# Far degree factors of every third chunk fetched from a table in HBM by GpSimd, in two of three sum stages of a graph kernel

## The chip, the cores and the metric

The program runs on one core of a Trainium2 chip. The metric is the device time of one execution in microseconds (us). The core has five engines with in-order instruction streams: TensorE (PE), VectorE (DVE), ScalarE (ACT), GpSimd (POOL) and SyncE (SP). SP issues plain DMAs; POOL issues the indirect ones (gathers and scatters by a list of row numbers). Engines wait for each other on semaphores.

## The reference

Two graph layers over 100000 nodes of 64 features and 25000 edges, sorted by destination. The part around the change is the second one, `_L1_gnn_ref`, called with `row = src`, `col = dst`:

```
for l in range(3):
    f1 = relu(x[row] @ nb_W[l] + nb_b[l]);  f2 = relu(x[col] @ self_W[l] + self_b[l])
    h = relu(concat([f1, f2]) @ att1_W[l] + att1_b[l])
    mask = clip(sigmoid(h @ att2_W[l] + att2_b[l]) * (ZETA - GAMMA) + GAMMA, 0, 1)
    rowsum = segment_sum(mask, row) + 1e-6
    d_inv_sqrt = clip(rowsum ** -0.5, 0, 10)
    vals = mask * d_inv_sqrt[row] * d_inv_sqrt[col]
    x = segment_sum(vals[:, None] * x[col], row)
    out = out + x
```

The factor `d_inv_sqrt[row]` is local to an edge once the edges stand in the order of `row`. `d_inv_sqrt[col]`, the far degree factor, stands at another place of the list and has to be looked up for each edge; where `col` has no edge of its own the factor is 10.

## The kernel before

The 25000 edges, padded to 25088, stand in 196 tiles of 128 edges, and four tiles make a chunk, so that there are 49 chunks (`NC1 = 49`, `C = 4`). For each of the three layers l = 0, 1, 2 there are three stages in a row:

- a dense stage (the matmuls of f1, f2 and h). For l = 1 and 2, POOL first gathers the rows of the last layer's `x`, 196 indirect DMAs at L1003, behind the semaphore `table`; the copy of the 100000 nodes to the output is done beside it in steps (`RUN_B`, `RUN_C`);
- a short chain for `rowsum` and its root, on 98 partitions by 256 places (`rowsum_dve`, L1206 to L1262). `DEGR` holds the 25088 degree factors by place. It is split at L1251 to L1259 into three bf16 parts, `TAB`, whose sum is the float;
- the sum stage (`aggregate_dve`), over the 49 chunks. The change lies here, for l = 0 and 1.

The sum stage looks the far factors up with TensorE. For each chunk c these steps follow one another:

- spread (SP, L1058): a DMA broadcasts the table row numbers of the chunk's 512 edges to all partitions, into one of two buffers `RB`;
- hot (ACT, L1355 and L1357): two activations turn them into a one-hot matrix `OH`, one of two buffers;
- bring (PE, L1451): 12 matmuls, four tiles by three parts, bring each edge's table row of 256 factors into PSUM;
- select (DVE, L1271): four instructions, one per tile, pick the column and leave the factor in `DCc`; the product with the near part is at L1274 (`VAL1`), and L1278 multiplies the chunk's feature rows by it (`Z`);
- turn_z (PE, L1461), scan (DVE, L1285, a running sum by segment), turn_back (PE, L1476), rows (ACT, L1348, a copy to SBUF) and store (SP, L1062, to HBM).

Each engine goes through its own list in order, with lags written out by `staged`: in step i, PE does bring(i), turn_z(i-2), turn_back(i-3); DVE does select(i), scan(i-2); ACT does hot(i), rows(i-4); SP does spread(i), store(i-5). So a spread stands behind a store on SP, and that store waits for rows, which stands behind a hot on ACT. In the first sum stage POOL does only one thing: it zeroes the chunk's part of `far` when the chunk is done (L999, 49 times); in the second and third sum stage before the change it has nothing there until the output scatters of the third (L1010). Below, T stands for the start of a chunk's select on DVE.

Of the kernel before, what the change touches and what calls it, by code (L numbers as in the profile page):

```python
# [9 lines left out]
ALU = mybir.AluOpType  # L10
# [17 lines left out]
C = 4  # L28
NCH = T // C
# [27 lines left out]
USE_DST = 0  # L57
NOROW = SL1 + 256
# [25 lines left out]
def build(nc, a, out):  # L84
    ctx = ExitStack()
    with ctx:
# [24 lines left out]
        row_d = dram("row_of_far_degree", (1, SL1), BF16)  # L111
        same_d = dram("same_as_before", (1, SL1), BF16)
# [863 lines left out]

        FORWARD, REVERSED = list(range(NC1)), list(range(NC1))[::-1]
# [7 lines left out]
        def L1_pool(g, top):  # L985
# [35 lines left out]
        def L1_sp(sp):  # L1021
# [31 lines left out]
            for l in range(LAYERS):  # L1053
                def spread(c, l=l):
                    b = c % 2
                    if l or c >= 2:
                        sp.wait_ge(signal("o_hot"), l * NC1 + c - 1)
# [13 lines left out]
                if l < 2:  # L1071
                    staged(NC1, [(0, spread), (5, store)])
# [133 lines left out]
        def rowsum_dve(v, l):  # L1206
# [42 lines left out]
            if l:  # L1249
                v.wait_ge(signal("o_mm"), NC1 * l)  # L1250
# [13 lines left out]
        def aggregate_dve(v, l):  # L1264

            def select(c):
                b = c % 2
                v.wait_ge(signal("o_mm"), l * NC1 + c + 1)
                for k in range(C):
                    u = C * c + k  # L1270
                    v.scalar_tensor_tensor(PICK[k], steps[:, :], far_c[:, u:u + 1], bank[2 + 2 * b + k // 2][:, (k % 2) * 256:(k % 2) * 256 + 256],  # L1271
                                           ALU.is_equal, ALU.mult, accum_out=DCc[:, u:u + 1])
                v.drain()  # L1273
# [34 lines left out]
        def L1_act(s_):  # L1308

            for l in range(LAYERS):  # L1310
# [39 lines left out]
                def hot(c, l=l):  # L1350
                    b = c % 2
                    s_.wait_ge(signal(f"o_ids{b}"), half_need(b, l, c))
                    if c >= 2:
                        s_.wait_ge(signal("o_mm"), l * NC1 + c - 1)
# [5 lines left out]
        def L1_pe(pe):  # L1360
# [27 lines left out]
            for l in range(LAYERS):  # L1388
# [53 lines left out]
                def bring(c, l=l):  # L1442
                    b = c % 2
# [3 lines left out]
                    if c >= 2:  # L1447
                        pe.wait_ge(signal("o_val"), l * NC1 + c - 1)
# [455 lines left out]
```

## Time and profile before

| | |
|---|---|
| median of 3 runs | 3198.88 us (3198.11 to 3206.03) |
| the profiled execution | 3199.13 us, span 3197.3 us |
| busy share of the span | DVE 69%, POOL 60%, PE 56%, PE weight load 45%, ACT 33% |
| chain that ended last | POOL 48%, issue 18%, DVE 13%, PE 12% |
| first sum stage | from about 2011 to about 2158 us |
| second sum stage | from about 2464 to about 2611 us |

The span is a sequence of stages with different limits, so these shares are an average. The chain of waits says which engine ended each stretch: POOL's indirect DMAs through the dense stages and the last sum stage, DVE through the first two sum stages, where its pieces return every 3 us. A row of a timeline gives start, duration, engine, line, operation, what it writes and reads, and in brackets how long its engine was idle before it and for whom.

### The profile page before, as it was taken

How to read it: one execution, taken by the hardware profiler on the slowest of the kernel's cores; microseconds unless marked ns; L12 is line 12 of the kernel's file. 1: busy time of each engine (PE TensorE's matmuls, PEld its weight loads, DVE VectorE, ACT ScalarE, POOL GpSimd, SP SyncE). 2: the span in 40 equal slices, each digit the busy share in tenths (PEclk: the TensorE clock that was granted, in tenths of full speed). 3: DMA queues.
4: the chain of work that ended last, by engine and by line, in shares of the span. 5: the costliest groups of instructions: out<-in, count | busy, mean ns of one | idle time of the engine just before them, and what ended most of it. 6: DMA issues, size and time to landing. Idle time of an engine off the chain costs nothing.

```text
span 3197.3 us, 34323 instructions
## 1 busy us (share of the span) xinstructions
PE 1780.0 (56%) x8972; PEld 1443.3 (45%) x8972; DVE 2195.2 (69%) x5951; ACT 1068.3 (33%) x2292; POOL 1913.7 (60%) x1844
## 2 busy tenths in 40 slices
PE   1124444441399986653665654665665656655663
PEld 0023333331299975542454433453444544544442
DVE  6748888887877744434555553897866988766775
ACT  0024444442144420001333323553444644443221
POOL 0057777777888017776777775017773017773776
PEclk9975555565555555556777776897888987787555
DMA  0023332231122212214222211233332333333543
GB/s 7 3 54 82 84 88 82 83 86 41 41 86 86 83 60 69 71 50 96 62 63 61 64 40 34 70 85 96 98 104 64 88 88 94 102 98 84 126 119 85
DMA packets 283933, 238.03 MB, mean 74 GB/s; under 512 B 161125, under 2 KB 207611, under 8 KB 283637
## 3 DMA queue, kind: packets, MB, share of 16 engines
q1 hardware_dynamic: 226933, 196.13, 21.4%
q0 software_dynamic: 56832, 40.05, 5.5%
q8 instruction: 58, 0.95, 0.1%
q14 instruction: 110, 0.90, 0.1%
HBM read 163.62 MB, written 84.20 MB: 78 GB/s over the span
## 4 chain that ended last, share of the span: by engine, by line
POOL 48%; issue 18%; DVE 13%; PE 12%; DVEq 4%; DMA 2%; SPq 1%; ACT 1%; POOLq 0%; ACTq 0%
POOL big L1003 13%; POOL G L994 12%; POOL regs L1845 7%; POOL out L1010 6%; POOL regs L1854 5%; PE bank L923 5%; POOL x_after_layer L647 5%; DVE den L1271 3%; PE bank L916 3%; DVE big L1285 2%; DVE big L1591 2%; PE bank L872 1%; DVEq L1590 1%; PE bank L1451 1%; DVEq L1273 1%
## 5 line engine op out<-in xcount | busy, mean ns | idle before, releaser
L1003 POOL DMA_INDIRECT big<-layer_rows,late x392 | 425.9, 1087 | 305.8 <-SPq L1075 186.9
L1845 POOL DMA_INDIRECT regs<-in_x,G x200 | 213.8, 1069 | 234.8 <-DVEq L1711 174.1
L1451 PE MATMUL bank<-regs,SQ 99*128 99x256 bf16 x1764 | 274.8, 319 | 84.2 <-ACT SQ L1357 77.7
L647 POOL DMA_INDIRECT x_after_layer<-G,idx_s x200 | 197.0, 985 | 198.0 <-DVEq L808 135.9
L1870 POOL DMA_INDIRECT farf<-dst_float,VAL x196 | 252.8, 1290 | 59.7 <-issue 59.7
L1451 PEld LDWEIGHTS bank<-regs,SQ 99*128 99x128 bf16 x1764 | 189.3, 112 | 152.8 <-ACT SQ L1357 102.7
L1010 POOL DMA_INDIRECT out<-G,scat_i x196 | 194.7, 993 | 104.4 <-issue 61.4
L1854 POOL DMA_INDIRECT regs<-in_x,G x200 | 211.2, 1056 | 70.2 <-issue 59.7
L1271 DVE SCALAR_TENSOR_TENSOR den<-steps,late,bank 128x256 f32<-128x256 f32 x588 | 245.2, 472 | 9.6 <-PE bank L1451 9.3
L994 POOL DMA_INDIRECT G<-x_after_layer,own_i x196 | 200.6, 1023 | 69.2 <-issue 61.0
L994 POOL DMA_INDIRECT G<-x_after_layer,far_i x196 | 198.5, 1013 | 66.5 <-issue 66.5
L505 PE MATMUL bank<-regs 128*128 128x196 bf16 x800 | 161.2, 356 | 90.8 <-ACT regs L492 90.8
L1355 ACT ACTIVATE SQ<-XC,row_of 128x512 bf16<-128x512 bf16 x147 | 105.9, 721 | 259.4 <-DMA XC<-row_of_far_degree 235.6
L1402 PE MATMUL bank<-ident,big 128*128 128x128 f32 x196 | 50.3, 347 | 226.8 <-DMA big<-layer_rows,late 226.8
L1398 PE MATMUL bank<-ident,XC 128*128 128x128 f32 x196 | 50.3, 408 | 215.2 <-DVEq L1114 215.2
L564 ACT ACTIVATE SQ<-XC 128x512 f32<-128x512 f32 x99 | 62.3, 629 | 284.8 <-DVE XC L547 284.7
L395 DVE RECIPROCAL dstat<-dstat 128x8 f32<-128x8 f32 (+1 forms) x196 | 38.9, 198 | 169.8 <-ACT dstat L408 169.8
L885 PE MATMUL bank<-ident,VS 128*128 128x128 f32 x100 | 32.6, 426 | 212.5 <-DVE VS L717 212.5
L933 PE MATMUL bank<-big,den 128*128 (+1 forms) x400 | 95.8, 420 | 93.4 <-DVE den L587 86.5
L1402 PEld LDWEIGHTS bank<-ident,big 128*128 128x128 f32 x196 | 23.2, 166 | 271.1 <-issue 270.9
L933 PEld LDWEIGHTS bank<-big,den 128*128 128x128 f32 x400 | 87.3, 322 | 106.7 <-issue 99.4
L1398 PEld LDWEIGHTS bank<-ident,XC 128*128 128x128 f32 x196 | 33.0, 206 | 226.0 <-issue 226.0
(416 smaller groups left out, 5745.7 us busy)
## 6 DMA issues: line engine op xcount, KB each, us to landing
regs<-x_after_layer SPq DMA_DIRECT2D x96, 256.0 KB, 3.2
out<-regs SPq DMA_DIRECT2D x96, 256.0 KB, 2.1
XC<-row_of_far_degree SPq DMA_DIRECT2D x147, 128.0 KB, 3.4
den<-in_x SPq DMA_DIRECT2D x50, 256.0 KB, 2.7
x_after_layer<-den SPq DMA_DIRECT2D x50, 256.0 KB, 2.0
regs<-tile_nodes SPq DMA_DIRECT2D x50, 256.0 KB, 3.2
layer_rows<-TS SPq DMA_DIRECT2D x98, 128.0 KB, 2.0
regs<-in_x SPq DMA_DIRECT2D x46, 256.0 KB, 2.8
```

The lines of the kernel that those rows point to most:

```text
L505: pe.matmul(o_, GE[b][h][:, k * P:(k + 1) * P], LT[:, h, part, :], start=(h + part == 0), stop=False)
L647: g.indirect_dma_start(x1_d, bass.IndirectOffsetOnAxis(ap=idx_s[:, b, k:k + 1], axis=0), G[:, b, k, 0, :], None, bounds_check=top, oob_is_ ...
L923: ins = pe.matmul(bank[4 + b][:, k * F:(k + 1) * F], ZTs[b][:, q * 512 + k * P:q * 512 + (k + 1) * P], wm[:, q, :], start=(q == 0), stop=( ...
L933: ins = pe.matmul(bank[b][:, k * F:(k + 1) * F], STg[b][:, k, :], big1[:, one(c, k), :].rearrange("p o f -> p (o f)"), start=True, stop=True)
L994: g.indirect_dma_start(G[:, b, grp // 2, grp % 2, :], None, x1_d, bass.IndirectOffsetOnAxis(ap=ix[:, u:u + 1], axis=0), bounds_check=top, ...
L1003: ahead(g, l, REVERSED, lambda u, l=l: g.indirect_dma_start(far[:, tile_of(u // C, u % C), :], None, xt_d[l - 1], bass.IndirectOffsetOnAxi ...
L1010: g.indirect_dma_start(out, bass.IndirectOffsetOnAxis(ap=scat_i[1][:, u:u + 1], axis=0), SUM[b][:, k, :], None, bounds_check=top, oob_is_e ...
L1271: v.scalar_tensor_tensor(PICK[k], steps[:, :], far_c[:, u:u + 1], bank[2 + 2 * b + k // 2][:, (k % 2) * 256:(k % 2) * 256 + 256], ALU.is_e ...
L1451: ins = pe.matmul(bank[2 + 2 * b + k // 2][:, (k % 2) * 256:(k % 2) * 256 + 256], OH[b][0:RB1 + 1, k * P:(k + 1) * P], TAB[0:RB1 + 1, part ...
L1845: g.indirect_dma_start(GR[:, c % DEEP, k, 0, :], None, a["x"], bass.IndirectOffsetOnAxis(ap=own0[:, c * C + k:c * C + k + 1], axis=0), bou ...
L1854: g.indirect_dma_start(GR[:, c % DEEP, k, 1, :], None, a["x"], bass.IndirectOffsetOnAxis(ap=far0[:, c * C + k:c * C + k + 1], axis=0), bou ...
L1870: g.indirect_dma_start(farf[:, u:u + 1], None, dstf_d, bass.IndirectOffsetOnAxis(ap=perm1[:, u:u + 1], axis=0), bounds_check=top, oob_is_e ...
```

## The change

For l = 0 and 1, chunks 5, 8, 11, ..., 47 (15 of the 49, `FETCHED`) are no longer looked up with TensorE. SP writes `DEGR` to a table in HBM once per layer (`table_out`, two DMAs behind `r_val`); POOL fetches from it by edge, with one indirect DMA of 128 single floats per tile (`fetch_degrees`, 60 per stage), at most three chunks in flight, and writes them into `DCc`. Places that have no factor keep the 10 that POOL writes there before. For a fetched chunk SP leaves out the spread, ACT the hot, PE the bring and DVE the four instructions of the select; the product at L1274 waits for the fetch (`pair0` to `pair2`) in place of the matmuls. The remaining 34 looked-up chunks alternate between the two buffers by a count of their own, `g`.

```
+FETCHED = [[c for c in range(NC1) if l < 2 and c >= 5 and c % 3 == 2] for l in range(3)]
+LOOKED = [[c for c in range(NC1) if c not in FETCHED[l]] for l in range(3)]
+LOOKED_BEFORE = [sum(len(LOOKED[k]) for k in range(l)) for l in range(4)]
...
+            def fetch_degrees(l):
+                g.wait_ge(signal("tables_out"), 16 + 32 * (l + 1))
+                for c in FETCHED[l]:
+                    i = fetch_index(l, c)
+                    landed = signal(f"pair{i % FARS}")
+                    if i >= FARS:
+                        g.wait_ge(landed, fetch_need(i - FARS))
+                    for u in range(C * c, C * c + C):
+                        g.indirect_dma_start(DCc[:, u:u + 1], None, deg_d, bass.IndirectOffsetOnAxis(ap=pos_i[:, u:u + 1], axis=0),
+                                             bounds_check=places, oob_is_err=False).then_inc(landed, 16)
...
+            for c in FETCHED[0]:
+                g.memset(DCc[:, C * c:C * c + C], 10.0)
+            g.drain()
+            fetch_degrees(0)
             for c in range(NC1):
                 g.wait_ge(signal("z_done"), c + 1)
                 g.memset(far[:, C * c:C * c + C, :], 0.0)
...
+                if l < 2:
+                    fetch_degrees(l)
...
+                def table_out(l=l):
+                    sp.wait_ge(signal("r_val"), l + 1)
+                    for h in range(2):
+                        sp.dma_start(at(deg_d, 256 * h, [[512, 49], [1, 256]]), DEGR[49 * h:49 * h + 49, :]).then_inc(signal("tables_out"), 16)
                 def spread(c, l=l):
-                    b = c % 2
-                    if l or c >= 2:
-                        sp.wait_ge(signal("o_hot"), l * NC1 + c - 1)
+                    if c not in LOOKED[l]:
+                        return
+                    g = LOOKED_BEFORE[l] + LOOKED[l].index(c)
+                    b = g % 2
+                    if g >= 2:
+                        sp.wait_ge(signal("o_hot"), g - 1)
...
-                    staged(NC1, [(0, spread), (5, store)])
+                    staged(NC1, [(0, spread), (1, lambda c: table_out() if c == 0 else None), (5, store)])
...
             def select(c):
                 b = c % 2
-                v.wait_ge(signal("o_mm"), l * NC1 + c + 1)
...
+                if c in FETCHED[l]:
+                    i = fetch_index(l, c)
+                    v.wait_ge(signal(f"pair{i % FARS}"), fetch_need(i))
+                else:
+                    g = LOOKED_BEFORE[l] + LOOKED[l].index(c)
+                    v.wait_ge(signal("o_mm"), g + 1)
...
                 def bring(c, l=l):
-                    b = c % 2
+                    if c not in LOOKED[l]:
+                        return
...
-                    pe.wait_ge(signal("o_hot"), l * NC1 + c + 1)
-                    if c >= 2:
-                        pe.wait_ge(signal("o_val"), l * NC1 + c - 1)
+                    pe.wait_ge(signal("o_hot"), g + 1)
+                    if i >= 2:
+                        pe.wait_ge(signal("o_val"), l * NC1 + LOOKED[l][i - 2] + 1)
```

The instruction streams show it on three engines. On VectorE, in the first sum stage (`den`, `late` and `VAL` are the buffers of the select and its product, `big<-big` or `big<-regs` the scan), from the select of chunk 4 on, before:

```order
L1271 SCALAR_TENSOR_TENSOR den,late<-steps,late,bank 128x256 [waits o_mm]
L1271 SCALAR_TENSOR_TENSOR den,late<-steps,late,bank 128x256 x3
L1274 TENSOR_TENSOR VAL<-late,VAL 128x4
L1278 TENSOR_TENSOR den<-big,VAL 128x256 [waits z_t]
L1285 SCALAR_TENSOR_TENSOR big<-regs,big,bank 128x256 [waits z_t,s_scan]
L1271 SCALAR_TENSOR_TENSOR den,late<-steps,late,bank 128x256 [waits o_mm]
L1271 SCALAR_TENSOR_TENSOR den,late<-steps,late,bank 128x256 x3
L1274 TENSOR_TENSOR VAL<-late,VAL 128x4
L1278 TENSOR_TENSOR den<-big,VAL 128x256 [waits z_t]
L1285 SCALAR_TENSOR_TENSOR big<-regs,big,bank 128x256 [waits z_t,s_scan]
```

and now, with chunk 5 in second place (the same instructions have the lines L1311, L1314, L1318 and L1325):

```order
L1311 SCALAR_TENSOR_TENSOR den,late<-steps,late,bank 128x256 [waits o_mm]
L1311 SCALAR_TENSOR_TENSOR den,late<-steps,late,bank 128x256 x3
L1314 TENSOR_TENSOR VAL<-late,VAL 128x4
L1318 TENSOR_TENSOR den<-big,VAL 128x256 [waits z_t]
L1325 SCALAR_TENSOR_TENSOR big<-regs,big,bank 128x256 [waits z_t,s_scan]
L1314 TENSOR_TENSOR VAL<-late,VAL 128x4 [waits pair0]
L1318 TENSOR_TENSOR den<-big,VAL 128x256 [waits z_t]
L1325 SCALAR_TENSOR_TENSOR big<-regs,big,bank 128x256 [waits z_t,s_scan]
```

The four selects of a fetched chunk are gone, and its product waits for `pair0`.

On SP, once the stage is full, a spread (the DMA into `XC`) and a store (the DMA to `layer_rows`) took turns before:

```order
L1062 DMA layer_rows<-TS 128x4x64 [waits q_out]
L1058 DMA XC<-row_of_far_degree 128x512 [waits o_hot]
L1062 DMA layer_rows<-TS 128x4x64 [waits q_out]
L1058 DMA XC<-row_of_far_degree 128x512 [waits o_hot]
L1062 DMA layer_rows<-TS 128x4x64 [waits q_out]
L1058 DMA XC<-row_of_far_degree 128x512 [waits o_hot]
```

and now:

```order
L1093 DMA XC<-row_of_far_degree 128x512 [waits o_hot]
L1097 DMA layer_rows<-TS 128x4x64 [waits q_out]
L1093 DMA XC<-row_of_far_degree 128x512 [waits o_hot]
L1097 DMA layer_rows<-TS 128x4x64 [waits q_out] x2
L1093 DMA XC<-row_of_far_degree 128x512 [waits o_hot]
L1097 DMA layer_rows<-TS 128x4x64 [waits q_out]
```

Two spreads in three steps remain, and the first of each pair stands behind two stores in place of one.

On ACT, a hot (two rows into `SQ`) and a rows (into `TS`) took turns. Now, from the hot of chunk 6 on, where a fetched chunk leaves two rows side by side:

```order
L1398 ACTIVATE SQ<-XC,row_of 128x512 [waits o_mm,o_ids0]
L1400 ACTIVATE SQ<-SQ,one_c 128x512
L1388 ACTIVATE TS<-bank 128x2x2x64 [waits q_stored1,s_bt]
L1388 ACTIVATE TS<-bank 128x2x2x64 [waits q_stored0,s_bt]
L1398 ACTIVATE SQ<-XC,row_of 128x512 [waits o_mm,o_ids1]
L1400 ACTIVATE SQ<-SQ,one_c 128x512
L1388 ACTIVATE TS<-bank 128x2x2x64 [waits q_stored1,s_bt]
```

The rows of every chunk keep their place behind a hot, while a third of the hots are gone.

## Rows read from the trace of the kernel before

**Rows 1.** Busy us (xcount) by stretch: PE, PEld, DVE, ACT, POOL; PEclk; DMA share; GB/s
```profile
2030.00:2140.00 110.00, 74.46 (x587) 57.01 (x584) 103.78 (x403) 66.08 (x110) 11.52 (x37) 1.00 0.39 89
2185.00:2425.00 240.00, 144.73 (x514) 106.71 (x513) 180.94 (x302) 103.65 (x257) 187.75 (x172) 0.84 0.33 100
2500.00:2600.00 100.00, 67.70 (x527) 52.30 (x525) 93.66 (x364) 59.84 (x99) 0.00 (x0) 0.98 0.38 88
2960.00:3160.00 200.00, 131.75 (x618) 91.76 (x616) 152.23 (x533) 54.84 (x76) 151.67 (x153) 0.56 0.49 123
```

**Rows 2.** Timeline of DVE, one chunk of the first sum stage
```profile
2071.06 0.45 DVE L1271 SCALAR_TENSOR_TENSOR den<-steps,late,bank 128x256 f32<-128x256 f32 x1
...
2072.80 0.16 DVE L1274 TENSOR_TENSOR VAL<-late,VAL 128x4 f32<-128x4 f32 x1
...
2074.06 0.45 DVE L1271 SCALAR_TENSOR_TENSOR den<-steps,late,bank 128x256 f32<-128x256 f32 x1
```

**Rows 3.** Timelines of PE, ACT and SP from the same point on
```profile
2071.19 0.44 PE L1476 MATMUL bank<-ident,big 128*128 128x128 f32 x2 [1.03 <-DVE big L1285]
2071.54 1.49 PE L1451 MATMUL bank<-regs,SQ 99*128 99x256 bf16 x12
...
2071.67 0.39 ACT L1348 ACTIVATE TS<-bank 128x256 f32<-128x256 f32 x1 [0.19 <-PE bank L1476]
...
2072.50 0.51 SPq L1058 DMA_DIRECT2D XC<-row_of_far_degree  x1
...
2075.93 0.72 ACT L1355 ACTIVATE SQ<-XC,row_of 128x512 bf16<-128x512 bf16 x1 [0.71 <-DMA XC<-row_of_far_degree]
```

**Rows 4.** Waits of ACT, 2010 to 2160 us: total, times, longest
```profile
ACT SQ L1355 <- DMA XC<-row_of_far_degree: 37.9, 41, 1.6
```

**Rows 5.** Timelines of ACT, PE and SP around a late spread
```profile
2142.54 0.72 ACT L1355 ACTIVATE SQ<-XC,row_of 128x512 bf16<-128x512 bf16 x1 [1.54 <-DMA XC<-row_of_far_degree]
...
2144.11 1.62 PE L1451 MATMUL bank<-regs,SQ 99*128 99x256 bf16 x12 [0.53 <-ACT SQ L1357]
...
2144.77 0.51 SPq L1058 DMA_DIRECT2D XC<-row_of_far_degree  x1
...
2148.25 0.72 ACT L1355 ACTIVATE SQ<-XC,row_of 128x512 bf16<-128x512 bf16 x1 [1.00 <-DMA XC<-row_of_far_degree]
```

**Rows 6.** Timelines of DVE and PE near the stage's start
```profile
2022.53 0.48 DVE L1271 SCALAR_TENSOR_TENSOR den<-steps,late,bank 128x256 f32<-128x256 f32 x1 [0.35 <-PE bank L1451]
...
2023.13 2.77 PE L1451 MATMUL bank<-regs,SQ 99*128 99x256 bf16 x12
...
2025.94 0.48 DVE L1271 SCALAR_TENSOR_TENSOR den<-steps,late,bank 128x256 f32<-128x256 f32 x1 [0.31 <-PE bank L1451]
...
2026.21 1.48 PE L1451 MATMUL bank<-regs,SQ 99*128 99x256 bf16 x12
```

**Rows 7.** POOL by line: busy us, mean ns, idle before
```profile
L1870 POOL DMA_INDIRECT farf<-dst_float,VAL x196 | 252.8, 1290 | 59.7 <-issue 59.7
L1003 POOL DMA_INDIRECT big<-layer_rows,late x187 | 204.0, 1091 | 57.0 <-issue 57.0
L999 POOL MEMSET big<- 128x256 f32 x49 | 15.3, 311 | 164.1 <-DVE den L1278 164.1
```

**Rows 8.** DVE by line and shape: first sum stage, then third
```profile
L1278 DVE TENSOR_TENSOR den<-big,VAL 128x256 f32<-128x256 f32 x30 | 12.7, 424 | 2.8
...
L1278 DVE TENSOR_TENSOR den<-big,VAL 128x256 f32<-128x256 f32 x40 | 17.2, 431 | 4.0 <-issue 0.4
```

**Rows 9.** DMA issues: KB each, median us to landing; first, then third stage
```profile
XC<-row_of_far_degree SPq DMA_DIRECT2D x31, 128.0 KB, 3.3
...
XC<-row_of_far_degree SPq DMA_DIRECT2D x40, 128.0 KB, 3.4
```

**Rows 10.** Timeline of DVE, end of the rowsum chain and first select
```profile
2006.21 0.42 DVE L1248 TENSOR_TENSOR den<-den 98x256 f32<-98x256 f32 x1
...
2011.41 0.48 DVE L1271 SCALAR_TENSOR_TENSOR den<-steps,late,bank 128x256 f32<-128x256 f32 x1 [2.42 <-PE bank L1451]
```

More of the change, by code:

```diff
@@ L111, in build @@
         row_d = dram("row_of_far_degree", (1, SL1), BF16)
+        deg_d = dram("degree_of_place", (SL1, 1))
         same_d = dram("same_as_before", (1, SL1), BF16)
@@ L975, in ahead_done, with fetch_index, fetch_need @@
                 eng.wait_ge(signal(f"ring{k}"), ROWS_IN + (16 * C) * ((use + 1) * len(range(k, NC1, RING))))
+        def fetch_index(l, c):
+            return l * len(FETCHED[0]) + FETCHED[l].index(c)
+        def fetch_need(i):
+            return 16 * C * (len(range(i % FARS, NCH, FARS)) + i // FARS + 1)
         FORWARD, REVERSED = list(range(NC1)), list(range(NC1))[::-1]
@@ L1249, in rowsum_dve @@
             if l:
-                v.wait_ge(signal("o_mm"), NC1 * l)
+                v.wait_ge(signal("o_mm"), LOOKED_BEFORE[l])
             v.tensor_copy(TAB[0:RB1, 0, :], DEGR)
@@ L1267, in select @@
                 b = c % 2
-                v.wait_ge(signal("o_mm"), l * NC1 + c + 1)
[L1269 to L1273, printed above, removed]
+                if c in FETCHED[l]:
[4 more added lines that the diff above has]
+                    v.wait_ge(signal("o_mm"), g + 1)
+                    for k in range(C):
+                        u = C * c + k
+                        v.scalar_tensor_tensor(PICK[k], steps[:, :], far_c[:, u:u + 1], bank[2 + 2 * (g % 2) + k // 2][:, (k % 2) * 256:(k % 2) * 256 + 256],
+                                               ALU.is_equal, ALU.mult, accum_out=DCc[:, u:u + 1])
+                    v.drain()
                 v.tensor_tensor(VAL1[:, C * c:C * c + C], DCc[:, C * c:C * c + C], VAL0[:, C * c:C * c + C], ALU.mult).then_inc(signal("o_val"), 1)
@@ L1350, in hot @@
                 def hot(c, l=l):
-                    b = c % 2
-                    s_.wait_ge(signal(f"o_ids{b}"), half_need(b, l, c))
-                    if c >= 2:
-                        s_.wait_ge(signal("o_mm"), l * NC1 + c - 1)
+                    if c not in LOOKED[l]:
+                        return
+                    g = LOOKED_BEFORE[l] + LOOKED[l].index(c)
+                    b = g % 2
+                    s_.wait_ge(signal(f"o_ids{b}"), 16 * (g // 2 + 1))
+                    if g >= 2:
+                        s_.wait_ge(signal("o_mm"), g - 1)
                     s_.activation(OFF[b], RB[b], ACT.Square, bias=row_of[:, 0:1])
@@ L1442, in bring @@
                 def bring(c, l=l):
-                    b = c % 2
+                    if c not in LOOKED[l]:
+                        return
+                    i = LOOKED[l].index(c)
+                    g = LOOKED_BEFORE[l] + i
+                    b = g % 2
                     if c == 0:
                         pe.wait_ge(signal("r_carry"), 2 * l + 2)
-                    pe.wait_ge(signal("o_hot"), l * NC1 + c + 1)
-                    if c >= 2:
-                        pe.wait_ge(signal("o_val"), l * NC1 + c - 1)
+                    pe.wait_ge(signal("o_hot"), g + 1)
+                    if i >= 2:
+                        pe.wait_ge(signal("o_val"), l * NC1 + LOOKED[l][i - 2] + 1)
                     for k in range(C):
@@ L1819, in _ @@
             top = g.to_reg(N - 1)
+            places = g.to_reg(SL1 - 1)
             for o in range(2):
@@ L1876, in _ @@
             L0_pool(g, top)
-            L1_pool(g, top)
+            L1_pool(g, top, places)
 mid_side, end_side = [], []
```

2 lines of the change are left out of this document (1 added, 1 removed).

## The prediction

> **What bounds the kernel now.** I read the busy time by stretch first, then the timelines of the five engines over two or three chunks, then the waits. In the first and second sum stage DVE is busy 94% of the time (103.78 of 110 us, 93.66 of 100) and TensorE's granted clock is 1.00 and 0.98, that is, 2.4 GHz nearly throughout [rows 1] (the stretches there are the first sum, a dense, the second sum and the third sum stage). One chunk takes DVE from 2071.06 to 2074.06, 3.00 us: 1.74 us for the select, up to the start of the product at 2072.80, and 1.26 us for the product, Z and the scan [rows 2]. The reader is to see in these rows that DVE has no gap to speak of, so that whatever leaves it counts at once. But ACT waits for the spread's DMA 41 times, 37.9 us in all [rows 4]: the next limit is near. The stages are passed in series (the dense stage starts on `table`, once the last store of the sum stage has landed), so a gain in a sum stage goes through to the end in full.
>
> **What the change removes.** For each fetched chunk DVE loses the 1.74 us of the select. Three chunks would then take 9.00 - 1.74 = 7.26 us. 15 fetched chunks in two stages make 30 x 1.74 = 52 us if DVE stayed the limit. That is the upper bound of the gain.
>
> **What is late next.** I follow the other engines' lists. Three loops matter, all prices at 2.4 GHz.
>
> Loop one, over three chunks. The spread of chunk c goes out on SP behind the store of c-6, and its rows waits for the scan that ends as the select of c-3 starts. From T at 2071.06, turn_back starts at 2071.19, rows at 2071.67, the spread goes out at 2072.50 (1.44 us after T), and its hot starts at 2075.93, 3.43 us later [rows 3]. From the start of a hot to that of its bring are 1.57 us (2142.54 to 2144.11) [rows 5], the bring takes 1.49 us [rows 3], and the select starts 0.04 us behind it (2023.13 + 2.77 = 2025.90 against 2025.94) [rows 6]. Sum: 1.44 + 3.43 + 1.57 + 1.49 + 0.04 = 7.97 us for three chunks. It is hidden today under 9.00, with 1.03 us to spare. Under 7.26 it isn't: the change leaves this loop as it is, since each looked-up chunk still stands behind the store of six chunks before.
>
> Loop two, over the hots. That same rows stands behind a hot on ACT, whose spread may be late. For the looked-up chunk that follows a fetched one, c-6's rows stands behind the hot of c-2. From that hot to this one it is 5.71 us where nothing else holds (2142.54 to 2148.25, through the rows, the store and the spread at 2144.77) [rows 5]. With the sequence looked A, looked B, fetched: B's hot starts at the earliest 1.44 + 3.43 = 4.87 us after the T of the B before; the next A's hot 5.71 us after it; that A's select 1.57 + 1.49 + 0.04 = 3.10 us later; the B behind it 3.00 us later. That is twice the period: 4.87 + 5.71 + 3.10 + 3.00 = 16.68 us, so 8.34 us for three chunks. The late spreads (5.71 already has one of 3.48) make me take 8.4.
>
> Loop three, on PE alone: a bring starts behind the turn_back of its step, 0.48 us after T (2071.06 to 2071.54) [rows 2, 3], so a looked-up chunk's T comes at least 0.48 + 1.49 + 0.04 = 2.01 us after the T before it. 3.00 + 3.00 + 2.01 = 8.01 us: below loop two at 2.4 GHz.
>
> So the stage goes from 9.00 to 8.4 us for three chunks and DVE gets 1.1 us of idle time: 15 x 0.6 = 9 us. Once per stage a lead is used up as well: the hot at 2075.93 [rows 3] is today 4.13 us ahead of its select, due three chunks after 2071.06, at 2080.06, and needs 3.10. That is 1.03 us: 10 us, 20 us for both.
>
> **TensorE's clock.** At 1.2 GHz the bring takes 2.77 us in place of 1.49, and the chunk lasts from 2022.53 to 2025.94, 3.41 us [rows 6]. With one in three fetched: 3.41 + 3.00 + 3.41 = 9.82 us, more than the 9.00 of today at 2.4 GHz. What will the clock do? PE is busy 74.46 of 110 us (2.03 us of a chunk) at 1.00; then 3 x 2.03 - 1.49 = 4.6 of 8.4 us, 55%. The dense stage has 60% busy at a clock of 0.84, the third sum stage 66% at 0.56, part of it stretched by the lower clock itself [rows 1]. After these the price is between a clock of 1.00 (8.4 us) and the third stage's 0.56 (12% of the time at 2.4 GHz: 9.6 us). I take 0.93, half way between first and dense stage: 86% of the time at 2.4 GHz. 1 / (0.86/8.4 + 0.14/9.82) = 8.57 us. Gain per stage: 15 x 0.43 + 1.03 = 7.5 us; both: 15 us.
> The Trainium skill ("TensorE: Matmul & The Clock Gate", section "A second HAM failure mode: psum-queue depth-cycling") says that an engine which idles briefly and often between groups of matmuls has its clock go up and down. The dense stage agrees; the first sum stage at 1.00, with its short pauses in every chunk, doesn't. By it the third case below would be the one.
>
> **What the change adds.** POOL's fetches: the same form, single floats by index, costs 1.290 us and 0.305 us of idle at L1870, wider rows at L1003 1.091 + 0.305 [rows 7]. At 1.595 a fetched chunk costs POOL 6.4 us (5.6 by the other), less than 7.26 or 8.4. The table: `r_val` comes at 2006.63 [rows 10]; two issues, 0.5 us each, and a landing of up to 3.4 us (rows 9 for a larger DMA) give 2011; the first four fetches are issued by 2017.4 and landed by 2021, while chunk 5, at 2025.94 today [rows 6], needs them then. Each later one gains on DVE. Cost nothing; if POOL took over 8.4 us a chunk, each us above would cost 30 us. SP holds the third spread back for about 1 us behind the table; the hot that it feeds waits for the first bring anyway (select 0 starts at 2011.41, 5 us after `r_val`) [rows 10]. POOL's 49 memsets of 0.31 us [rows 7] come late in the first stage: fetches end by 2011 + 15 x 6.4 = 2107, the backlog of some 30 by 2120, before the stage ends. In the second stage POOL is free. Shared DMA engines: in the third stage, with POOL's scatters beside it and a DMA share of 0.49, a spread lands in 3.4 against 3.3 us [rows 1, 9]: 0 to 0.1 us on either loop, 0 to 3 us in all, inside my 8.4.
> DVE beside a busy POOL: Z takes 431 ns in the third stage against 424 [rows 8], nothing with DVE no longer the limit. The Trainium skill ("GPSIMD Engine Reference", section 8, key points) says that POOL shares its SBUF interfaces with VectorE, with contention where an instruction has two inputs in SBUF, as Z has. The trace bounds that at 7 ns here; by rule or row the sum stays within 1 us.
>
> **The sum.** 3199.13 us of the profiled execution - 15 = 3184 us; the median of the runs, 3198.88, is the same to 0.01%.
>
> **The rivals.**
> 1. DVE stays the limit. For it: 94% busy. Against: loops one and two, which would both have to be shorter, by spreads that land in some 2.4 us. Its full time is 3147; part of it (loop one alone: about 8.0 us, 1.0 x 15 = 15 us per stage) gives 3169.
> 2. The clock falls as in the dense stage, 0.84: 68% at 2.4 GHz, 8.80 us, (0.20 x 15 + 1) x 2 = 8 us: 3191, and a little lower clock gives none: 3191 to 3205, which can't be told from no change. For it: 55% busy. Against: at 1.2 GHz two brings of 2.77 us alone fill 5.5 of 9.8 us, and in the stretch of rows 6 the clock was back by the bring at 2026.21, 1.48 us.
> 3. Slower: PE at 1.2 GHz for most of both stages. Its place is the bring behind a turn_back, its price 9.6 to 9.82 us for three chunks, 8 to 11 us per stage lost: 3215 to 3221. It decides from where the share at 2.4 GHz falls below half: 1 / (0.5/8.4 + 0.5/9.82) = 9.05. For it: the third sum stage, at 0.56 with the same matmuls.
> 4. The fetches come late (the change doesn't do what it says): needs more than 8.4 us per four on POOL, against 6.4 in the rows. At 10 us a stage would be bound at 10 us for three chunks: 3229.
>
> **Numbers.** Forecast (8.3 to 8.7 us for three chunks) 0.48, its own range 3177 to 3190; rival 1 0.13, rival 2 0.24, rival 3 0.11, rival 4 0.04. Predicted 3184 us. The range 3164 to 3204 takes in the forecast, the near part of rival 1 and nearly all of rival 2. A measurement here tells a change from none above about 0.3%, 9.6 us: faster 0.60, same 0.25, slower 0.15.
>
> **What would show it.** In the profile after: a select-to-select time over three chunks of 8.3 to 8.6 us with DVE idle about 1 us in each, ahead of the looked-up chunk's select and put down to PE's bring; ACT still waiting for the spread's DMA; the product at its new line never waiting for a fetch; POOL 6.4 us per fetched chunk; a clock above 0.9 in both stages; dense and third stages as long as before. A period of 7.3 us, or a wait of DVE for `late`, would show the loops or the fetch wrong; a clock below 0.8, my reading of the clock.

## The result, and the profile after

| | before | after |
|---|---|---|
| median of the runs, us | 3199.63 (18 runs, 3192.61 to 3206.47) | 3211.06 (18 runs, 3202.38 to 3220.01) |
| profiled execution, us (span) | 3199.13 (3197.3) | 3212.64 (3210.8) |
| first sum stage, first select to end fix, us | 149.21 | 156.01 |
| second sum stage | 149.47 | 157.09 |
| third sum stage | 251.86 | 252.34 |

The change makes the kernel slower: ratio 1.0033, 95% interval 1.0024 to 1.0042, about 11 us. The forecast was 3184 us. The two stages that were changed lost 6.8 and 7.6 us, together 14.4 us, and the span grew by 13.5: what happened is in these two stages. (Stage lengths here and below are read from the timeline of VectorE, from its first select to the fix at the stage's end.)

The windows of the profile after, the same four stretches as in [rows 1]: first sum, dense, second sum, third sum. The columns are those of [rows 1].

```profile
2030.00:2140.00 110.00, 77.69 (x412) 57.75 (x411) 81.01 (x289) 46.64 (x82) 53.91 (x85) 0.70 0.31 70
2185.00:2425.00 240.00, 156.61 (x511) 115.62 (x512) 182.20 (x303) 104.59 (x255) 187.59 (x173) 0.76 0.33 100
2500.00:2600.00 100.00, 70.60 (x377) 52.69 (x378) 71.86 (x256) 42.79 (x74) 32.86 (x33) 0.72 0.31 70
2960.00:3160.00 200.00, 126.27 (x608) 88.69 (x608) 153.03 (x536) 54.36 (x77) 151.59 (x153) 0.60 0.49 123
```

DVE fell from 94% busy to 74% (81.01 of 110 us), as the change wants. PE runs 412 instructions where it ran 587, and yet it is busy longer, 77.69 us against 74.46. The column that explains it is the clock: 1.00 became 0.70, and 0.98 became 0.72. Fewer matmuls, each slower. The page's rows of the bring and the select say the same over the whole kernel:

```profile
L1498 PE MATMUL bank<-regs,SQ 99*128 99x256 bf16 x1404 | 278.1, 377 | 89.8 <-ACT SQ L1400 83.6
...
L1311 DVE SCALAR_TENSOR_TENSOR den<-steps,late,bank 128x256 f32<-128x256 f32 x468 | 196.4, 475 | 73.8 <-PE bank L1498 73.3
```

1764 matmuls of the bring became 1404, and their busy time rose from 274.8 to 278.1 us, 319 to 377 ns each. The select, hardly ever waiting before (9.6 us in all), now has 73.8 us of idle time ahead of it, put down to the bring.

The waits from 2010 to 2160 us (total, times, longest):

```profile
PE bank L1523 <- DVE VAL L1314: 35.3, 15, 2.7
DVE den L1311 <- PE bank L1498: 33.2, 22, 2.4
ACT SQ L1398 <- DMA XC<-row_of_far_degree: 25.5, 29, 1.6
```

The first row is the one to look for. PE's turn_back waits for DVE 15 times, once per fetched chunk, 2.35 us each. (The wait is put down to the product; what turn_back needs is the scan three chunks back, which ends as that product starts.) PE is not idle for longer in all: from about the sixth chunk to the last it is idle for 41 of 129 us before (in 51 pauses, the longest 1.03 us) and for 40 of 139 us after (in 24 pauses, 12 of them over 2.2 us). The timeline shows it in one group of three chunks. PE, DVE and ACT, start and duration, the idle time before in brackets:

```profile
2046.05 0.48 DVE L1311 SCALAR_TENSOR_TENSOR den<-steps,late,bank 128x256 f32<-128x256 f32 x1 [2.08 <-PE bank L1498]
...
2046.66 2.55 PE L1498 MATMUL bank<-regs,SQ 99*128 99x256 bf16 x12
...
2049.25 0.48 DVE L1311 SCALAR_TENSOR_TENSOR den<-steps,late,bank 128x256 f32<-128x256 f32 x1
...
2049.27 0.38 PE L1523 MATMUL bank<-ident,big 128*128 128x128 f32 x2
...
2049.49 0.38 PE L1508 MATMUL bank<-ident,den 128*128 128x128 f32 x2
...
2052.07 0.72 ACT L1400 ACTIVATE SQ<-SQ,one_c 128x512 bf16<-128x512 bf16 x1
...
2052.27 0.14 DVE L1314 TENSOR_TENSOR VAL<-late,VAL 128x4 f32<-128x4 f32 x1
...
2052.41 0.69 PE L1523 MATMUL bank<-ident,big 128*128 128x128 f32 x2 [2.54 <-DVE VAL L1314]
...
2052.89 2.77 PE L1498 MATMUL bank<-regs,SQ 99*128 99x256 bf16 x12
...
2055.69 0.48 DVE L1311 SCALAR_TENSOR_TENSOR den<-steps,late,bank 128x256 f32<-128x256 f32 x1 [2.11 <-PE bank L1498]
```

At 2049.87 PE has done all it can: the next chunk is a fetched one and has no bring, and turn_back waits for the scan behind four selects. 2.54 us later it starts again, and now its 12 matmuls take 2.77 us instead of 1.49 [rows 3], the duration of [rows 6] at 1.2 GHz. DVE waits 2.11 us for them. The clock over the pause and over the bring behind it (columns as in [rows 1]):

```profile
2049.87:2052.41 2.54, 0.00 (x2) 0.01 (x1) 2.37 (x10) 1.26 (x3) 1.93 (x3) 0.97 0.45 96
2052.89:2055.66 2.77, 2.77 (x14) 2.08 (x14) 0.69 (x2) 1.83 (x3) 2.16 (x3) 0.50 0.33 68
```

The full clock stands in the pause, where PE does nothing, and the low one in the bring. A mean clock of 0.70 over the stage is therefore too kind to the bring: it takes 2.39 us on average in both stages, nearer to 2.77 than to 1.49.

From select to select over three chunks: 2055.69 - 2046.05 = 9.64 us; before it was 9.00. Over all groups from chunk 4 on the mean is 9.55 us in the first stage and 9.54 in the second. The chain of waits between 2040 and 2060 us, by line, before and then after:

```profile
by line: DVE den L1271 40.4%; DVE big L1285 25.9%; issue 14.0%; DVEq L1273 13.0%; DVE VAL L1274 4.9%; DVE den L1278 2.2%; DVEq L1277 1.4%
```
```profile
by line: PE bank L1498 50.7%; DVE den L1311 20.9%; PE bank L1523 11.1%; DVEq L1317 9.6%; PE bank L1508 4.3%; issue 2.6%; DVE VAL L1314 2.3%; DVEq L1313 1.9%; DVE den L1318 0.6%
```

The chain was all DVE, apart from issue; it is two thirds PE now. POOL's fetches are in time: the product never waits for one. In 2000 to 2170 us,

```profile
L1005 POOL DMA_INDIRECT late<-degree_of_place,late x60 | 60.0, 1000 | 49.2 <-DMA degree_of_place<-den 31.2 <-issue 18.0
```

so 1.00 + 0.30 us each, 5.2 us per fetched chunk.

### The profile page after: what moved, and what is told of

The parts are those of the page before. It is cut to its first block, busy times and chain, and to the rows that moved or that the text cites. A ratio compares the mean times of both kernels' runs of the same rounds, so it can differ in the third digit from the quotient of the medians.

```text
span 3210.8 us, 33298 instructions
## 1 busy us (share of the span) xinstructions
PE 1790.6 (56%) x8612; PEld 1447.0 (45%) x8612; DVE 2149.0 (67%) x5711; ACT 1026.9 (32%) x2232; POOL 2036.6 (63%) x1979
## 4 chain that ended last, share of the span: by engine, by line
POOL 48%; issue 17%; PE 15%; DVE 11%; DVEq 4%; DMA 3%; SPq 1%; ACT 1%; POOLq 0%; ACTq 0%
POOL big L1028 13%; POOL G L1015 12%; POOL regs L1893 7%; POOL out L1037 6%; POOL regs L1902 5%; PE bank L927 5%; POOL x_after_layer L651 5%; PE bank L1498 4%; PE bank L920 3%; DVE den L1311 2%; DVE big L1638 2%; PE bank L876 1%; DVEq L1637 1%; PE bank L1523 1%; DMA XC<-row_of_far_degree 1%
## 5 line engine op out<-in xcount | busy, mean ns | idle before, releaser
L1498 PE MATMUL bank<-regs,SQ 99*128 99x256 bf16 x1404 | 278.1, 377 | 89.8 <-ACT SQ L1400 83.6
L1498 PEld LDWEIGHTS bank<-regs,SQ 99*128 99x128 bf16 x1404 | 180.3, 133 | 172.4 <-ACT SQ L1400 106.5
L1311 DVE SCALAR_TENSOR_TENSOR den<-steps,late,bank 128x256 f32<-128x256 f32 x468 | 196.4, 475 | 73.8 <-PE bank L1498 73.3
L1005 POOL DMA_INDIRECT late<-degree_of_place,late x120 | 119.7, 998 | 90.3 <-DMA degree_of_place<-den 54.3
L1445 PE MATMUL bank<-ident,big 128*128 128x128 f32 x196 | 53.0, 363 | 219.7 <-DMA big<-layer_rows,late 219.6
L1398 ACT ACTIVATE SQ<-XC,row_of 128x512 bf16<-128x512 bf16 x117 | 84.3, 721 | 235.2 <-DMA XC<-row_of_far_degree 219.0
L1523 PE MATMUL bank<-ident,big 128*128 128x128 f32 x294 | 83.9, 382 | 98.5 <-DVE VAL L1314 71.0
```

The costliest lines, as they stand in the source:

```text
L1005: g.indirect_dma_start(DCc[:, u:u + 1], None, deg_d, bass.IndirectOffsetOnAxis(ap=pos_i[:, u:u + 1], axis=0), bounds_check=places, oob_is_ ...
L1498: ins = pe.matmul(bank[2 + 2 * b + k // 2][:, (k % 2) * 256:(k % 2) * 256 + 256], OH[b][0:RB1 + 1, k * P:(k + 1) * P], TAB[0:RB1 + 1, part ...
```

## The experiments

The theory after the result: the brings that went away leave PE a pause of 2.5 us once in three chunks; TensorE's clock falls to 1.2 GHz for most of the stage; and as the bring behind the pause lies on the path, three chunks take 9.6 us. Rivals: POOL's fetches and their DMAs slow the rest; loops one and two are longer than thought; it isn't the brings, but the shorter work of DVE. One table gives what the traces showed (stage lengths as above; clock in one window per sum stage, from about the sixth chunk to the last), then each experiment. Each row's lengths and clocks come from one profiled execution, and the whole of such an execution differs from the median of its kernel by up to 12 us (with the stores on ScalarE 3193.93 us against 3205.76, with the extra matmuls 3197.55 against 3187.87); so a difference of a few us in one stage length is weak by itself. Ratios are against runs of the kernel before on the same chip.

| kernel | ratio (95%) | sum 1, us | sum 2, us | granted clock |
|---|---|---|---|---|
| before | 1 | 149.21 | 149.47 | 0.99, 0.99 |
| after | 1.0033 (1.0024 to 1.0042) | 156.01 | 157.09 | 0.70, 0.72 |
| 12 extra matmuls in the pause | 0.9965 (0.9952 to 0.9978) | 141.65 | 148.32 | 0.97, 0.92 |
| no fetches | 1.0029 (1.0016 to 1.0042) | 152.64 | 153.94 | 0.76, 0.74 |
| fetches alone | 1.0009 (0.9998 to 1.002) | 150.65 | 151.23 | 0.97, 0.99 |
| selects kept | 1.0047 (1.0032 to 1.0062) | 155.01 | 157.24 | 0.77, 0.71 |
| stores on ScalarE | 1.0027 (1.0015 to 1.0039) | 151.53 | 154.75 | 0.75, 0.72 |
| extra matmuls and stores on ScalarE | 0.9909 (0.9895 to 0.9922) | 132.87 | 135.04 | 1.00, 0.99 |

**Extra matmuls in the pause.** Once per fetched chunk PE does 12 matmuls of the bring's shape into a bank that the next bring overwrites; nothing reads them.

```
+                def warm(c, l=l):
+                    if c in FETCHED[l]:
+                        ...
+                        for k in range(WARM):
+                            pe.matmul(bank[...][:, 0:256], TAB[0:RB1 + 1, 0, 0:P], TAB[0:RB1 + 1, 0, :], start=True, stop=True)
-                staged(NC1, [(0, bring), (2, turn_z), (3, turn_back)])
+                staged(NC1, [(0, bring), (2, turn_z), (0, warm), (3, turn_back)])
```

> The changed kernel with 12 extra matmuls (bf16, 256 columns, into the PSUM bank that the next bring overwrites, result unused) in each fetched chunk's step on TensorE, between turn_z and turn_back, where TensorE sits idle for about 2.5 us in the changed kernel. Clock theory (the pause lowers the clock to 1.2 GHz and the bring behind it, 2.77 us, is then on the path): clock in the sum stages at 0.9 or more, three chunks in 8.3 to 8.6 us in place of 9.6, first select to end of the first sum stage 140 to 144 us (before 149.2, changed 156.0), time 3180 to 3190 us. Contention theory (POOL's fetches slow the spreads or DVE): clock may rise, but three chunks stay at 9.4 us or more and the time at 3208 to 3213 us.

Measured: 3187.87 us, ratio 0.9965 (0.9952 to 0.9978) to the kernel before. More work on the engine that was the bound makes the kernel 23 us faster than the change as it was (3211.06 to 3187.87). PE in the second stage:

```profile
2518.62 1.48 PE L1517 MATMUL bank<-regs 99*128 99x256 bf16 x12
...
2521.12 0.44 PE L1531 MATMUL bank<-ident,big 128*128 128x128 f32 x2 [1.02 <-DVE VAL L1315]
```

The pause shown is 1.02 us, and the clock 0.97 in the first stage, 0.92 in the second. The bring of the first stage takes 281 ns per matmul against 377 (here and then after):

```profile
L1499 PE MATMUL bank<-regs,SQ 99*128 99x256 bf16 x348 | 44.9, 281 | 15.3 <-ACT SQ L1401 15.3
```
```profile
L1498 PE MATMUL bank<-regs,SQ 99*128 99x256 bf16 x348 | 69.3, 377 | 1.7 <-ACT SQ L1400 1.6
```

In the first stage 12 of 14 groups of three chunks take 8.1 to 8.6 us. In the second only 8 do; the others take 9.0 to 10.0, and 9 of 29 brings are slow there, though no pause is over 1.40 us. Since this kernel keeps the fetches, the spreads and DVE's shorter list, it shows that the clock cost what the change lost.

**No fetches.** POOL's fetches are left out and the product waits for none, the table is still written, and the factor 10 stands in for the values (DVE writes it once, in place of POOL).

```
                     for u in range(C * c, C * c + C):
-                        g.indirect_dma_start(DCc[:, u:u + 1], None, deg_d, ...).then_inc(landed, 16)
+                        pass
...
-                    v.wait_ge(signal(f"pair{i % FARS}"), fetch_need(i))
+                    pass
```

> The changed kernel without POOL's fetches from the table (the table is still written; the factor 10 stands in for the fetched ones). Clock theory: as the changed kernel, clock about 0.70 in the sum stages, about 9.5 us for three chunks, 3208 to 3213 us. Contention theory: three chunks fall to 8.4 to 9.0 us and the time to 3185 to 3200 us.

Measured: 1.0029 (1.0016 to 1.0042), not to be told from the kernel after, and a clock of 0.76 and 0.74. In the traces the stages are some 3 us shorter than after (152.64 and 153.94). Without a single fetch the loss is there: the rival "fetches" falls as the main cause on this chip, and keeps some 3 us a stage in the traces (3.4 and 3.2), 2 us in all by the medians (3209.14 against 3211.06).

**Fetches alone.** The kernel before, with the table and 60 fetches per stage into a tile that nobody reads.

```
-FETCHED = [[c for c in range(NC1) if l < 2 and c >= 5 and c % 3 == 2] for l in range(3)]
+FETCHED = [[] for l in range(3)]
+WANTED = [[c for c in range(NC1) if l < 2 and c >= 5 and c % 3 == 2] for l in range(3)]
```

> All chunks are looked up with TensorE as before the change; the table is written and POOL makes the same 60 fetches per stage, into a tile that nobody reads. Clock theory: no difference from before, 3196 to 3203 us, clock 0.98 to 1.00 in the sum stages, 3.00 us per chunk. Contention theory: spreads land later than 3.3 to 3.4 us or DVE's instructions last longer, and the time rises by 10 us or more.

Measured: 1.0009 (0.9998 to 1.002), 3203.28 us, stages 1.4 and 1.8 us longer than before, clock 0.97 and 0.99. So the fetches cost under 2 us per stage where DVE is the limit, nearly all of it in one group of three chunks (10.36 and 10.60 us; most others take 9.0), and they hardly touch the clock.

**Selects kept.** As after, but DVE does four selects for each fetched chunk all the same, on the bank of the chunk before; their sums go nowhere. PE's bring also waits for them before it overwrites that bank.

```
+                    for k in range(C):
+                        v.scalar_tensor_tensor(PICK[k], steps[:, :], ..., bank[2 + 2 * (j % 2) + k // 2][...],
+                                               ALU.is_equal, ALU.mult, accum_out=farf[:, u:u + 1])
```

> The changed kernel, but VectorE still does the four select instructions of a fetched chunk (on the matmul results of the chunk before, its result unused), so that VectorE saves nothing and only the spread, hot and bring of every third chunk are gone. Clock theory (the missing brings alone bring the clock down): clock 0.65 to 0.80, a looked-up chunk 3.4 us at 1.2 GHz, 9.5 to 9.8 us for three chunks, 3208 to 3218 us, slower than before although no engine has more to do. Rival (the clock falls because VectorE's short step for a fetched chunk leaves TensorE waiting): clock 0.95 or more, 9.0 us for three chunks, 3197 to 3203 us.

Measured: 1.0047 (1.0032 to 1.0062), clock 0.77 and 0.71. The window of the first stage:

```profile
2024.00:2159.00 135.00, 91.01 (x512) 66.30 (x510) 123.04 (x472) 56.59 (x99) 59.94 (x94) 0.77 0.31 69
```

DVE has before's load again (91% busy) and the clock is still down. So it is the brings that PE no longer has, and not DVE's shorter list, that bring it down. Three chunks take 9.4 to 9.6 us with and without the selects, and the long pause stays (13 pauses over 2.2 us in this window): at this clock what DVE saves is worth next to nothing.

**Stores on ScalarE.** ScalarE issues the store behind its rows, so SP has the spreads alone and loop one is gone.

```
+                    s_.wait_ge(signal("q_out"), l * NC1 + c + 1)
+                    s_.dma_start(sums_of(xt_d[l], c), TS[:, b]).then_inc(signal(f"q_stored{b}"), 16)
-                    staged(NC1, [(0, spread), (1, ...), (5, store)])
+                    staged(NC1, [(0, spread), (1, ...)])
```

> The changed kernel with the store of each chunk issued by ScalarE right behind its rows copy, so that SyncE's list in the sum stages holds spreads alone and no spread stands behind a store. Clock theory: the clock stays at 0.65 to 0.80, a looked-up chunk stays at 3.4 us at 1.2 GHz, three chunks at 9.2 to 9.8 us, time 3203 to 3212 us. Loop theory (the spread behind the store is what holds the changed kernel back): three chunks at 8.0 us, time 3175 to 3185 us.

Measured: 1.0027 (1.0015 to 1.0039), clock 0.75 and 0.72, three chunks 9.2 to 9.4 us. The stages are 4.5 and 2.3 us shorter than after, but not under before's. Late spreads are a small part, as long as the clock is down.

**Both.** The extra matmuls and the stores on ScalarE.

> Both: 12 extra matmuls in the pause, and the stores issued by ScalarE. If the loops of the prediction are what is left once the clock is up, three chunks go from 8.4 us to 8.0 us, the loop on TensorE alone (3.00 + 3.00 + 2.01), the sum stages from 142 to 148 us to 135 to 140 us, time 3172 to 3182 us. If something else held the kernel with the extra matmuls (3188 us), no gain: 3185 to 3190 us.

Measured: 3170.15 us (6 runs, 3167.04 to 3175.28) against 3199.93; 0.9909 (0.9895 to 0.9922). The forecast was 3172 to 3182 us and 135 to 140 us per stage, so it came out a little better. This kernel beats the kernel before by 29 us and, by the two ratios, the kernel after by 40. Together the two edits are worth more (these 40 us against after) than the sum of each alone (22 and 2 us, worked out in the same way): each uncovers the limit that the other takes away. Its first stage:

```profile
2059.24 0.48 DVE L1312 SCALAR_TENSOR_TENSOR den<-steps,late,bank 128x256 f32<-128x256 f32 x1 [0.61 <-PE bank L1501]
...
2062.90 1.48 PE L1519 MATMUL bank<-regs 99*128 99x256 bf16 x12
...
2065.26 0.14 DVE L1315 TENSOR_TENSOR VAL<-late,VAL 128x4 f32<-128x4 f32 x1
...
2065.41 0.44 PE L1533 MATMUL bank<-ident,big 128*128 128x128 f32 x2 [1.03 <-DVE VAL L1315]
...
2065.68 1.48 PE L1501 MATMUL bank<-regs,SQ 99*128 99x256 bf16 x12
...
2067.19 0.48 DVE L1312 SCALAR_TENSOR_TENSOR den<-steps,late,bank 128x256 f32<-128x256 f32 x1 [0.61 <-PE bank L1501]
```

2067.19 - 2059.24 = 7.95 us: the prediction's loop three, 8.01 us; 25 of 28 groups take 7.9 to 8.1. DVE waits 0.61 us per three chunks, for the bring behind turn_back.

**The bring ahead of that turn_back.** As the last one, with turn_z and turn_back one step later, to take the bring off loop three.

```
-                staged(NC1, [(0, bring), (2, turn_z), (0, warm), (3, turn_back)])
+                staged(NC1, [(0, bring), (3, turn_z), (0, warm), (4, turn_back)] if l < 2 else ...)
```

> As the last, and in the first two sum stages TensorE does each bring one step earlier against turn_z and turn_back (lags 0, 3, 4 in place of 0, 2, 3), so that the bring no longer stands behind the turn_back of the step before. VectorE is then the limit: 7.3 to 7.5 us for three chunks, 127 to 132 us per sum stage, time 3158 to 3170 us. If TensorE's or the spreads' side still holds it: 8.0 us and 3172 to 3182 us.

Measured: 3334.78 us, 1.042 (1.0404 to 1.0437), a clear miss. One place shows why:

```profile
2058.90 2.74 PE L1501 MATMUL bank<-regs,SQ 99*128 99x256 bf16 x12 [2.49 <-ACT SQ L1403]
...
2061.44 0.64 PE L1511 MATMUL bank<-ident,den 128*128 128x128 f32 x2
...
2062.18 0.43 DVE L1319 TENSOR_TENSOR den<-big,VAL 128x256 f32<-128x256 f32 x1 [4.59 <-PE bank L1511]
```

DVE's Z of a chunk needs a buffer that turn_z frees, and turn_z now stands behind a bring, which waits for its hot, which stands on ACT behind rows, which waits for turn_back. The waits that ran beside each other run in a ring, some 14 us for three chunks (10.5 to 15.1).

**The same without the extra matmuls.**

```
-                staged(NC1, [..., (3, turn_z), (0, warm), (4, turn_back)] if l < 2 else ...)
+                staged(NC1, [..., (3, turn_z), (4, turn_back)] if l < 2 else ...)
```

> As the last, without the 12 extra matmuls. The bring in the pause fills it: if the pause is what lowers the clock, and not the smaller amount of matmul work, clock 0.9 or more and a time within 5 us of the last. If the smaller amount of work lowers it, clock 0.65 to 0.8 and three chunks at 8 to 9 us, 3175 to 3200 us, since the brings at 1.2 GHz are then partly ahead of VectorE.

Measured: 1.0435 (1.0417 to 1.0453). The bring did not fill the pause, and the order itself costs 4%, so the time says nothing. The clock does. The first stage with the extra matmuls, then without:

```profile
2030.00:2229.00 199.00, 126.27 (x694) 96.75 (x694) 99.19 (x365) 57.62 (x101) 61.83 (x96) 0.69 0.18 48
```
```profile
2030.00:2226.00 196.00, 118.67 (x517) 82.02 (x514) 98.77 (x363) 57.29 (x100) 59.42 (x94) 0.51 0.19 48
```

Both have 28 pauses over 2.2 us in this stretch, all but one of 2.5 us (the wait of the bring for its hot); the extra matmuls stand elsewhere, behind a turn_z, and take out only short waits of 0.4 us. With the same long pauses the clock is 0.69 with them and 0.51 without (0.70 and 0.51 in the second stage). So the length of the longest pause is not all that the clock answers to.

**How many matmuls, every second chunk, and the stores alone.** Four kernels: the best one with 6 and with 18 extra matmuls, the best one with every second chunk fetched, and the kernel before with the stores on ScalarE. They ran twice, on two chips.

```
-WARM = 12
+WARM = 6
```
```
-WARM = 12
+WARM = 18
```
```
-FETCHED = [[c for c in range(NC1) if l < 2 and c >= 5 and c % 3 == 2] for l in range(3)]
+FETCHED = [[c for c in range(NC1) if l < 2 and c >= 5 and c % 2 == 1] for l in range(3)]
```

6 matmuls: 

> 12 extra matmuls replaced by 6, stores on ScalarE. They fill 0.75 us of the pause in place of 1.5. If the clock hangs on how much of the pause is filled: clock between 0.76 (none, with the same stores) and 0.92 to 1.00 (12), time 3175 to 3200 us. If a few matmuls anywhere in the pause are enough: as with 12, 3168 to 3174 us.

18 matmuls: 

> 18 extra matmuls, 2.2 us at 2.4 GHz, stores on ScalarE. If they still fit within the pause: clock 0.97 or more in both sum stages, three chunks 8.0 to 8.2 us, 3166 to 3176 us. If they hold the turn_back behind them back: three chunks above 8.3 us, 3176 us or more.

Every second chunk: 

> Every second chunk from 5 on fetched (22 of 49 per stage), 12 extra matmuls in each fetched step, stores on ScalarE. If POOL becomes the limit as computed (4 x 1.30 = 5.2 us for a fetched chunk against TensorE's 3.00 + 2.01 = 5.01 us for two chunks): two chunks take 5.2 to 5.4 us, 3163 to 3175 us. If the clock falls again: clock below 0.85, 3180 to 3200 us.

Stores alone: 

> The kernel before the change, with only the stores of the first two sum stages moved to ScalarE. VectorE is the limit there: no difference, 3196 to 3203 us, 3.00 us per chunk. If the spread behind the store already cost time before: 3190 us or less.

Measured: on both chips the kernel before itself took 3907 and 3916 us, not 3200. The ratios there are 1.0379 (1.0222 to 1.0536), 1.0295 (1.0045 to 1.0546), 1.0419 (1.024 to 1.0598) and 0.9875 (0.9671 to 1.0079) in the second set; the first gave 1.0436 (1.0284 to 1.0589) for 6 matmuls, 1.0515 (1.0357 to 1.0672) for every second chunk, 1.0156 (1.0037 to 1.0276) for the stores alone, and for 18 matmuls 4039.96 us (3972.56 to 4057.82) without a ratio. So on these chips the three kernels with fetches are slower than the kernel before, by 3 to 5%; on the chip of 3200 us they didn't run, and the question of the fastest version stays open.

The traces show where the loss is. In each changed stage the product of chunk 6 comes 84 to 88 us behind the first select with 60 fetches and 123 us behind it with 88, where the best kernel takes 17 to 19 us on the chip of 3200 us. POOL's fetches last 60 x 1.30 = 78 and 88 x 1.30 = 114 us there. In that time the stage all but stands still (in the first stage with 6 matmuls, 2405 to 2435 us, PE is busy for 2.40 of 30 us and the DMA share is 0.04), with waits that the profile puts down to "remote". The kernel with the stores alone has no fetches, and its stages last 149 to 150 us, as they do before on the other chips. So on these two chips the rival "fetches" is the main cost; what the fetches hold up is not shown. (POOL's wait for the table, 32.3 us in one trace, is no sign of it: it is 31.2 us in the kernel after as well.)

What can be used for the clock is the part behind that start. One window each, for 6 matmuls, 18 matmuls and every second chunk:

```profile
2475.00:2588.00 113.00, 79.26 (x575) 61.91 (x573) 95.03 (x344) 54.18 (x96) 12.79 (x41) 0.91 0.31 78
```
```profile
2470.00:2579.00 109.00, 88.33 (x734) 71.99 (x731) 93.57 (x339) 52.32 (x94) 12.57 (x41) 1.00 0.34 81
```
```profile
2500.00:2600.00 100.00, 76.61 (x645) 65.00 (x643) 81.53 (x280) 44.17 (x80) 12.45 (x40) 0.98 0.31 77
```

With stores on ScalarE the granted clock of the two stages is 0.75 and 0.72 without extra matmuls, 0.91 and 0.88 with 6, 1.00 and 0.99 with 12 (on the chip of 3200 us), 1.00 and 1.00 with 18; three chunks take 9.2 to 9.4, about 8.3, 8.0 and about 8.0 us. The longest recurring pauses are 2.5, 1.7, 1.0 and 0.7 us. Six are not enough, and eighteen bring nothing over twelve. With every second chunk fetched, three chunks' worth takes about 7.4 us, and the kernel before with the stores alone keeps its 9.0 us: there DVE is the limit, and loop one is hidden.

## Why the prediction was wrong

It said 3184 us and a gain of 15 us; the kernel lost 11. By its own steps:

- **What bounds the kernel** (DVE at 94%, gains in a sum stage go through to the end): right. The changes of the two stages, 14.4 us, are the change of the span, 13.5 us, within 1 us.
- **What the change removes** (1.74 us per fetched chunk): right. The fetched chunk has only its product, Z and scan.
- **The three loops** (8.0, 8.3, 8.0 us for three chunks at 2.4 GHz): right where they could show. One group of three in the profile after, from 2065.38 to 2073.82 us, had a clock of 0.90 and took 8.44 us; with the clock held up most groups of the first stage take 8.1 to 8.6, where the prediction had 8.4; with the stores moved as well they take 7.95 to 8.0, which is loop three.
- **POOL's cost** (6.4 us per fetched chunk, nothing on the path): 5.2 us, and no wait of the product for a fetch, as forecast. Taken alone the fetches cost 1.4 to 1.8 us per stage, 3.2 us in all, where the prediction had 0 to 3 us in all for the shared DMA engines; beside the low clock some 3 us per stage. What of it is the table, the queue or the shared DMA engines wasn't separated.
- **TensorE's clock**: the step that failed. "I take 0.93, half way between first and dense stage" was 0.70 and 0.72. The bound was there, the third stage's 0.56, with 9.6 us for three chunks; 9.55 is what came. The argument against it was a busy share of 55%. But that share was computed at 2.4 GHz, and at the lower clock the same work filled 71% (77.69 of 110 us) without the clock staying up.
- **The average over the clock**, in the same step: the prediction mixed the periods at the two clocks by the mean granted clock. With the measured 0.70 that sum gives 1 / (0.40/8.4 + 0.60/9.82) = 9.20 us for three chunks, a loss of 15 x 0.20 - 1.03 = 2 us per stage and 3203 us in the end. Measured are 9.55 us and 3211. The full clock fell largely in pauses (0.97 in the pause shown), and the brings had 2.39 us on average. So the clock's level and this weighting both failed.

A row that bore on the question was the pause. Turn_back's wait, 1.03 us with a bring in front of it, grows by 1.49 us where the bring goes: 1.03 + 1.49 = 2.52 us; measured 2.54. That sum could have been made blind. And the trace of the kernel before has the fall of the clock as well. The prediction read in [rows 6] that the clock was back by the bring at 2026.21; the rows just ahead of [rows 6] show what went before:

```profile
2015.85 1.47 PE L1451 MATMUL bank<-regs,SQ 99*128 99x256 bf16 x12 [0.67 <-DVE VAL L1274]
...
2019.24 0.69 PE L1476 MATMUL bank<-ident,big 128*128 128x128 f32 x2 [1.69 <-DVE big L1285]
2019.72 2.77 PE L1451 MATMUL bank<-regs,SQ 99*128 99x256 bf16 x12
```

The clock was down behind a pause of 1.69 us, and it was back after PE had worked from 2019.24 to 2026.21 without any pause. The changed kernel has a longer pause in every 9.6 us.

The third rival had the place and the price: the bring behind a turn_back, 9.6 to 9.82 us for three chunks, 3215 to 3221 us. It had 0.11. The end came at 3211, a little below its range, as 9.55 us is a little below its 9.6: (15 x 0.55 - 1.03) x 2 = 14 us, by the prediction's own form of the sum. It was to decide once the share at 2.4 GHz fell below half, and the share was (0.70 - 0.5) / 0.5 = 40%.

The Trainium skill ("TensorE: Matmul & The Clock Gate", section "A second HAM failure mode: psum-queue depth-cycling") tells of a kernel whose TensorE idles briefly and often between groups of matmuls and whose clock goes up and down, and that spoke for this rival. The prediction set it aside because the first sum stage of the kernel before, with a short pause in nearly every chunk, held 1.00. Both stand: with pauses of up to 1.03 us in nearly every chunk the clock was up here, and with one of 2.5 us in three chunks and a third of the brings gone it was down most of the time.

What stays open: how the length of the pause and the amount of matmul work share in what the clock does. The change and the extra matmuls alter both at once. The two kernels with the bring ahead have the same long pauses and differ in the work, and their clocks differ by 0.18; a pair with the same work and other pauses wasn't run. Also open are what the fetches hold up on the chips of 3900 us, why the kernel before is slower there at all, and whether the best kernel gains more with every second chunk fetched on the other chips.

## What to carry to other kernels

When work is taken from TensorE to relieve another engine, work out the pause that it leaves in PE's list (old wait plus the work removed) and price the path at 1.2 GHz as well; a busy share alone hides it, and so does a mean clock, part of which falls in the pauses. Where the matmul behind the pause is on the path, filling the pause with matmuls that nobody reads can pay (12 of them per three chunks gave 0.7% back here). And when a limit is removed, look at the next two at the same time: the stores moved alone gave little, with the clock up they gave 18 us more.

## What the runs showed of the hardware

- TensorE at a mean granted clock of 1.00 with waits of up to 1.03 us in nearly every chunk of 3.00 us, and of 0.70 with one wait of 2.5 us in 9.6 us, while busy 71% of the time in the second case and 68% in the first. A higher busy share went with the lower clock.
- With the same pauses of 2.5 us, two in some 14 us, the clock was 0.69 with 12 more matmuls in those 14 us and 0.51 without.
- Inside a stage with a mean of 0.70 the clock was 0.97 over a pause and 0.50 over the bring behind it.
- An indirect DMA of 128 single floats costs POOL 1.00 us and 0.30 us of issue in this stage, against the 1.09 and 1.29 us of the other forms [rows 7].
- DVE's select took 475 ns in the first sum stage with POOL's fetches beside it and 470 before: 1%.
- On two chips the kernel before and the four of the last experiment took 3834 to 4101 us, where the kernel before takes 3200 on the others. With fetches, a sum stage all but stood still there while POOL made them (84 to 88 us to the product of chunk 6 with 60 fetches, 123 with 88); without them it took 149 us as elsewhere.
